# Conv, attention and a routed expert layer on one core: twelve row buffers, roots amid the scatters, the end in eight chunks, and an fp32 product a step that nothing reads

## What is computed

```python
t = t + _L1_attn_ref(_ln_t(t), ...)          # per image: softmax(q k^T / 8) v
t = t + _L1_ffn_ref(_ln_t(t), ...)

def _L1_ffn_ref(x, gate_w, gate_b, w1, w2, w3):
    probs = softmax(x @ gate_w + gate_b)     # 16 experts
    top_probs, top_idx = top_k(probs, 2)
    top_probs = top_probs / sum(top_probs)
    hidden = silu(x @ w1[e]) * (x @ w2[e])   # 64 -> 128, per expert e
    return sum over the two e: top_prob * (hidden @ w3[e])
```

## Time and profile before

| | |
|---|---|
| Median of 3 runs | 452.91 us (451.58 to 456.62) |
| The profiled execution | 452.74 us, span 450.9 |
| PE busy | 359.0 us (80% of the span) |
| DVE busy | 272.1 us (60%) |
| ACT busy | 183.2 us (41%) |
| POOL busy | 162.1 us (36%) |
| Granted PE clock, mean over the span | 0.813 |

### The profile page before, as it was taken

How to read it: one execution, slowest core, us unless ns; L and a number is a source line. 1 busy time by engine, 2 the same in 40 slices (tenths; PEclk the granted TensorE clock), 3 DMA queues, 4 the chain that set the end, 5 groups by cost and what they waited for, 6 DMA issues and landing times. The chain is left out here.

```text
span 450.9 us, 8512 instructions
## 1 busy us (share of the span) xinstructions
PE 359.0 (80%) x2739; PEld 193.0 (43%) x2739; DVE 272.1 (60%) x559; ACT 183.2 (41%) x409; POOL 162.1 (36%) x171
## 2 busy tenths in 40 slices
PE   1689999999999999999998478935507788788760
PEld 0543353433534435344341257735504455465540
DVE  3478977689777798787789656835402232233212
ACT  2683655646556565465630045430012233233220
POOL 2264223234222442224300120457652445445450
PEclk9978999999999999999999979965555555555555
DMA  8769998988978588395880000000023433343315
GB/s 257 312 145 214 287 223 260 302 218 204 221 176 216 128 191 218 76 223 129 195 228 0 1 0 2 9 19 25 24 66 74 94 87 94 91 98 82 94 33 140
DMA packets 55091, 61.50 MB, mean 136 GB/s; under 512 B 22900, under 2 KB 35244, under 8 KB 54928
## 3 DMA queue, kind: packets, MB, share of 16 engines
q1 hardware_dynamic: 45760, 54.30, 47.8%
q10 hardware_dynamic: 6768, 4.62, 3.9%
q0 software_dynamic: 2528, 2.14, 1.6%
HBM read 11.95 MB, written 11.83 MB: 53 GB/s over the span
## 5 line engine op out<-in xcount | busy, mean ns | idle before, releaser
L684 DVE TENSOR_TENSOR prod<-ps_t,a_rep 128x1024 f32<-128x1024 f32 x128 | 152.1, 1219 | 35.4 <-PE ps_t L384 29.3
L791 POOL TENSOR_TENSOR a<-a,mask 128x512 f32<-128x512 f32 (+1 forms) x40 | 46.8, 1171 | 84.3 <-ACT a L544 82.1
L384 PE MATMUL ps_t<-b,vt 32*128 32x512 f32 x512 | 74.7, 650 | 2.0 <-DVE prod L684 1.9
L404 PE MATMUL ps_d<-prod,keep 128*32 128x512 f32 x512 | 69.1, 611 | 1.2 <-DVE prod L684 0.9
L1254 POOL DMA_INDIRECT parts<-y_sb,x_in x47 | 46.0, 978 | 59.0 <-ACT y_sb L1353 42.9
L325 PEld LDWEIGHTS ps_m<-om_r,sel 128*128 128x128 f32 x193 | 29.0, 188 | 75.3 <-ACT mask L522 28.2
L325 PE MATMUL ps_m<-om_r,sel 128*128 128x256 f32 x193 | 49.3, 334 | 0.0
L1500 PE MATMUL ps_xv<-attention_pack,x_in 128*128 128x128 f32 x47 | 21.0, 446 | 31.5 <-DMA x_in<-rows 31.5
L1140 DVE COPY xs<-ps_xv 128x128 f32<-128x128 f32 x47 | 13.7, 291 | 45.7 <-PE ps_xv L1500 45.7
L768 POOL TENSOR_TENSOR om_r<-om_f,om_r 56x512 fp32r<-56x512 f32 x16 | 20.3, 1272 | 56.7 <-ACT om_r L511 56.6
L1345 ACT ACTIVATE gated<-ps_s 128x128 f32<-128x128 f32 x47 | 13.0, 278 | 62.2 <-PE ps_p L1509 62.2
(11 more groups left out here) (151 smaller groups left out, 494.3 us busy)
## 6 DMA issues: line engine op xcount, KB each, us to landing
a_rep<-a SPq DMA_DIRECT2D x128, 256.0 KB, 4.8
rows<-blank SPq DMA_DIRECT2D x8, 1056.0 KB, 7.4
w_in<-in_experts ACTq DMA_DIRECT2D x47, 96.0 KB, 2.0
a_rep<-a SPq DMA_DIRECT2D x32, 128.0 KB, 3.6
x_in<-rows SPq DMA_DIRECT2D x47, 33.0 KB, 1.9
x_in<-rows SPq DMA_DIRECT2D x47, 32.0 KB, 1.8
start<-in_start SPq DMA_DIRECT2D x1, 1344.0 KB, 7.8
both<-parts SPq DMA_DIRECT2D x4, 256.0 KB, 4.0
```

What stands on the lines that cost most here:

```text
L384: mm = pe.matmul(out, vt[par][r, v % 2, :, :, :].rearrange("p j y c -> p (j y c)"), b[par][r, pair_taps(v // 2), :].rearrange("p t x -> p ...
L404: mm = pe.matmul(ps_d[r, :], fold[:, v % 2, :], p, start=v == 0, stop=False, skip_group_check=True)
L684: dve.tensor_tensor(p[:, :, :], t[:, :, :], a_rep[par][:, ms, pair_taps(v // 2), :].rearrange("p m t x -> p m (t x)"), ALU.mult).then_inc( ...
L791: pool.tensor_tensor(v, v, mask[(PAIRS * par + k) % 2][:, 0:wide, :], ALU.mult).then_inc(a_done, 1)
```

## The change

1. `RING`, the number of buffers for rows (`x_in`) and results (`y_sb`) and of the semaphores `x_here` and `sent`, goes from 6 to 12. The weight buffers keep 6 under a name of their own, `WRING`.
2. POOL's `place(q)` becomes `place(q, half)` with four scatters in each half. `power(1, 2)` now stands between the halves of `place(0)`, `power(1, 3)` between those of `place(1)`.
3. The end goes by 8 chunks (`CHUNKS`) of two tiles (`HALF`) instead of 4 of four. SP loads and stores the even chunks, ACT the odd ones, which for that waits for all `sent` itself.
4. In `output(s)`, the wait for `y_done` comes first, then a new fp32 product of two constant tiles, `ident` and `ones` (128x128 each), into a part of PSUM that nothing reads (`ps_go_spare`), and only then the wait for `hidden_done` and the output's product.

```diff
-    RING = 6
+    RING, WRING = 12, 6
     LOADS = 4
+    CHUNKS = 2 * COUPLES
+    HALF = K // 2
...
+        ps_go_spare = [bank_go[:, b, 2 * P:3 * P] for b in two]
...
-            for q in range(COUPLES):
-                sp.dma_start(both[q][:, :, :, :], parts_view[:, K * q:K * (q + 1), :, :]).then_inc(both_in[q], 16)
-            for q in range(COUPLES):
-                sp.wait_ge(finished, q + 1)
-                sp.dma_start(out_view[:, K * q:K * (q + 1), :], t_tok[:, K * q:K * (q + 1), :]).then_inc(stored, 16)
-            sp.wait_ge(stored, 16 * COUPLES)
+            for c in range(0, CHUNKS, 2):
+                sp.dma_start(both[c][:, :, :, :], parts_view[:, HALF * c:HALF * (c + 1), :, :]).then_inc(both_in[c], 16)
+            for c in range(0, CHUNKS, 2):
+                sp.wait_ge(finished, c + 1)
+                sp.dma_start(out_view[:, HALF * c:HALF * (c + 1), :], t_tok[:, HALF * c:HALF * (c + 1), :])\
+                  .then_inc(stored, 16)
+            sp.wait_ge(stored, 16 * CHUNKS)
...
-                for k in range(K * q, K * (q + 1)):
+                for k in range(K * q + HALF * half, K * q + HALF * (half + 1)):
...
-            place(0)
+            place(0, 0)
             power(1, 2)
-            place(1)
+            place(0, 1)
+            place(1, 0)
             power(1, 3)
-            place(2)
-            place(3)
+            place(1, 1)
+            for q in (2, 3):
+                for half in two:
+                    place(q, half)
...
+            for b in range(RING):
+                act.wait_ge(sent[b], 16 * ((STEPS - 1 - b) // RING + 1))
+            for c in range(1, CHUNKS, 2):
+                act.dma_start(both[c][:, :, :, :], parts_view[:, HALF * c:HALF * (c + 1), :, :]).then_inc(both_in[c], 16)
+            for c in range(1, CHUNKS, 2):
+                act.wait_ge(finished, c + 1)
+                act.dma_start(out_view[:, HALF * c:HALF * (c + 1), :], t_tok[:, HALF * c:HALF * (c + 1), :])\
+                   .then_inc(stored, 16)
...
             def output(s):
-                b = s % RING
-                pe.wait_ge(hidden_done, s + 1)
+                b = s % WRING
                 if positive(s - 1):
                     pe.wait_ge(y_done, s - 1)
+                pe.matmul(ps_go_spare[s % 2], ident, ones, start=True, stop=True)
+                pe.wait_ge(hidden_done, s + 1)
                 pe.matmul(ps_y[s % 2], hidden[s % 2][:, :], w_in[b][:, HIDDEN:HIDDEN + C], start=True, stop=True)\
                   .then_inc(y_ps, 1)
```

More of the change, by code:

```diff
@@ L886, in token_stage @@
         x_in = [sb(f"x_in{b}", [P, C + ROW]) for b in range(RING)]
-        w_in = [sb(f"w_in{b}", [P, HIDDEN + C]) for b in range(RING)]
+        w_in = [sb(f"w_in{b}", [P, HIDDEN + C]) for b in range(WRING)]
         xs = [sb(f"xs{b}", [P, P]) for b in two]
@@ L891, in token_stage @@
         y_sb = [sb(f"y_sb{b}", [P, C]) for b in range(RING)]
-        both = [sb(f"both{b}", [P, K, 2, C]) for b in range(COUPLES)]
-        added = [sb(f"added{b}", [P, K, C]) for b in range(COUPLES)]
+        both = [sb(f"both{b}", [P, HALF, 2, C]) for b in range(CHUNKS)]
+        added = [sb(f"added{b}", [P, HALF, C]) for b in range(CHUNKS)]
         bank_xv, bank_s, bank_p, bank_go = ps("ps_xv"), ps("ps_s"), ps("ps_p"), ps("ps_go")
@@ L949, in token_stage @@
         x_here = [sem(f"x_here{b}") for b in range(RING)]
-        w_here = [sem(f"w_here{b}") for b in range(RING)]
+        w_here = [sem(f"w_here{b}") for b in range(WRING)]
         sent = [sem(f"sent{b}") for b in range(RING)]
@@ L958, in token_stage @@
         y_done = sem("y_done")
-        both_in = [sem(f"both_in{b}") for b in range(COUPLES)]
+        both_in = [sem(f"both_in{b}") for b in range(CHUNKS)]
         sum_done = sem("sum_done")
@@ L1151, in finish @@
                 dve.wait_ge(sum_done, q + 1)
-                tokens = t_tok[:, K * q:K * (q + 1), :]
+                tokens = t_tok[:, HALF * q:HALF * (q + 1), :]
                 dve.tensor_tensor(tokens, added[q][:, :, :], tokens, ALU.add).then_inc(finished, 1)
@@ L1219, in _ @@
                     hide(s + 1)
-            for q in range(COUPLES):
-                finish(q)
+            for c in range(CHUNKS):
+                finish(c)
         @block.gpsimd
@@ L1235, in power, with place @@
                     .then_inc(ln_pow[s], 1)
-            def place(q):
+            def place(q, half):
                 pool.wait_ge(staged, 2 * (q + 1))
@@ L1336, in weights_in @@
                     expert_rows.extend(table_values(act, 1, s, (EXPERTS - 1) * P))
-                if positive(s - RING + 1):
-                    act.wait_ge(y_ps, s - RING + 1)
+                if positive(s - WRING + 1):
+                    act.wait_ge(y_ps, s - WRING + 1)
                 act.dma_start(w_in[b][:, :], w_rows[bass.ds(expert_rows[s], P), :]).then_inc(w_here[b], 16)
@@ L1395, in _ @@
             gap_exps(3)
-            for s in range(RING - 1):
+            for s in range(WRING - 1):
                 weights_in(s)
@@ L1402, in _ @@
                 shared(s)
-                if s + RING - 1 < STEPS:
-                    weights_in(s + RING - 1)
+                if s + WRING - 1 < STEPS:
+                    weights_in(s + WRING - 1)
+            for b in range(RING):
[6 more added lines that the diff above has]
+                   .then_inc(stored, 16)
         @block.tensor
@@ L1502, in products @@
             def products(s):
-                b = s % RING
+                b = s % WRING
                 pe.wait_ge(xs_done, s + 1)
-                pe.wait_ge(w_here[b], 16 * uses(s))
+                pe.wait_ge(w_here[b], 16 * (s // WRING + 1))
                 if positive(s - 1):
```

## The result

| | before | after |
|---|---|---|
| Median | 453.97 us of 20 runs (450.62 to 457.30) | 446.46 us of 20 runs (445.18 to 451.97) |
| The profiled execution | 452.74 us, span 450.9 | 446.41 us, span 444.6 |
| Granted PE clock, mean over the span | 0.813 | 0.815 |

After stands to before as 0.984, 95% interval 0.982 to 0.987. The changed kernel is faster by 1.6%, where 8% had been forecast. The whole difference of 6.3 us between the two profiled executions can be laid out from rows.

What follows compares the result with a forecast made beforehand. The prediction took the six-buffer ring and PE at 1.2 GHz to bound the expert steps, with POOL next. Its sum was 452.74 - 33.1 (steps) - 3.5 (roots) - 1.0 (end) = 415.1 us, range 411 to 448.

Steps and rivals of the forecast that it cites:

- What bounds the kernel: Expert steps: six-buffer ring and PE's own work make 2.05 us a step; POOL is next at 1.28.
- Twelve row buffers: Expert steps: way round the ring falls to about 0.7 us a step, so row loads leave the path.
- The extra product's price: Each expert step on PE: 0.43 us at 1.2 GHz, 0.22 us at 2.4 GHz.
- Which level: Expert steps: the added product lifts PE's clock to 2.4 GHz, chance 0.52; steps stage -33.1 us.
- once up stays up: Expert steps: a risen PE clock holds, because the steps contain no long PE standstill.
- The pace once up: Expert steps at 2.4 GHz: POOL binds at 1.28 us a step, 58.9 us for 46 intervals.
- the forecast's 2.5 us for the rise: First 3.5 expert steps: still slow until the clock rises, 0.71 us each over POOL's pace.
- The forecast's sign of PE waiting for DVE ahead of L1533: Expert steps: PE waiting for DVE there would show the high-clock case right; no size given.
- Roots: POOL's scatters: roots placed between them remove its pauses; last scatter starts 3.5 us earlier.
- The end: After the last send: eight chunks on two queues save 1.0 us, bounds 0 and -2.
- The clock stays at 1.2 GHz: Rival for the expert steps: clock never rises, steps 1.99 us, 445.2 us in all; chance 0.30.
- Slower: Rival for the expert steps: clock stays low, product costs up to 0.87 us, 465 us; chance 0.06.

Runs made afterwards that it cites:

- the bridged kernel: Changed kernel plus 60 unread products on PE before the first step, three and two more behind the first two transposes: 414.53 us, 0.914 of before.
- the run with two and then one: Changed kernel with two unread products in each of the first ten steps, one in every later step: 421.10 us, 0.929 of before.
- the run with the burst and no product in the steps: Changed kernel with 52 unread products on PE ahead of the first step and none in the steps: 425.31 us, 0.941 of before.

## Why the prediction was right or wrong

- **What bounds the kernel: right.** Ring and PE shared the 2.05 us a step. With the ring taken away PE's own 1.55 us remains (the runs without the product and with the ring alone), as the earlier trace rows had it. One reading in it was off: the chain of the earlier trace rows comes round every four steps, not six, by the order told at the run with the product alone. 8.05 / 4 is 2.01 us a step, which explains the 2.05; 8.05 / 6 would be 1.34 and bind nothing. With twelve buffers it carries ten steps, 0.8 us each and not 0.7, still under 1.28.
- **Twelve row buffers: right where it counts.** At 1.2 GHz no transpose waits for rows after the first steps. At 2.4 GHz, where the same was forecast, the bridged kernel has two such waits left, 0.8 us in all; they cost nothing, as POOL still sends every 1.28 us.
- **The extra product's price: right.** 0.43 us forecast at 1.2 GHz, 19.7 us over 46 steps measured; the step is 1.985 us, forecast 1.99. At 2.4 GHz steps with none, one and two products go at PE's pace of 0.90, 1.13 and 1.35 us (starts in the timelines of the three kernels), so 0.22 us apiece as forecast; "about 1.0" for a step with one was 0.13 short, but below POOL's 1.28, so it moves nothing.
- **Which level: wrong, and this is the step that failed.** I wrote: "I think it goes up, as a little better than even." It stayed at 0.50 through all 90 us. The only rise I had seen came after nothing but dense products; I carried that over to a step which has 0.43 us of them in 1.99. The rows of before already had two full stretches at 0.50, and I read the new product as enough to change their mix. The waits for rows that broke the stretches did go, as forecast, and that didn't raise it either. In the runs it took two a step (0.86 us in 2.41), or a burst. The other half of the step, "once up stays up", was right, as the run with two and then one shows; but its rows (268 to 270 us with PE 1.45 of 2.00 busy) are rows of holding and say nothing of a kernel that first has to rise. In the sum, the term was -33.1 us and became -4.0.
- **The pace once up: right.** With the clock raised by a burst, the sends take 59.1 us, against 46 x 1.28 = 58.9 forecast, POOL binds, and the time is 414.5 us, against 415.1. That the totals agree so well is in part luck: the forecast's 2.5 us for the rise, which the bridged kernel has under its burst, and its 1.0 off the end, which isn't there, offset each other in part. The forecast's sign of PE waiting for DVE ahead of L1533 isn't there either: PE runs ahead of POOL (steps 1.13 us apart, sends 1.28), and from 345 to 400 us it waits 0.8 us for rows and not for DVE. The mechanism was right; the change as made doesn't set it off.
- **Roots: right.** 3.8 us less between first and last scatter, forecast 3.5; undone in the bridged kernel, 3.6.
- **The end: mis-sized.** -1.0 forecast, 0 measured. DVE's wait for the fifth chunk ends 5.43 us after the first load's issue, and that for the third couple had ended 5.63 us after it; DVE then needs 2.19 us for eight small operations where four large ones took 1.67, and the smaller store gives 0.3 back. The 0.3 us for a small operation was right (0.29, against 0.42 for 128x256), but the forecast counted only the last chunk's two, and eight stand behind DVE's last wait. It also took off half of the 2.04 us of issue; but each of the two queues still has four loads to issue. The Trainium skill (Trainium Kernel Development and Optimization, Key Constraints) says that a second issuing engine saves only issue time; the trace agrees as far as it goes: the landing stays, and two queues took 1.93 and 2.00 us for four loads each, as long as SP alone for four of twice the size (2.04), so what the second queue saved went into the doubled number of loads.
- **The rivals.** "The clock stays at 1.2 GHz" was given 445.2 us and a chance of 0.30; 446.46 was measured. Its own terms: steps -3.0 forecast, -4.0 measured (of which 0.7 because the last two sends are 1.28 us apart and not 1.99); roots -3.5, -3.8; end -1.0, 0.0; the other 1.5 us lie ahead of the first scatter and of the first send. "Slower" fell: switching between 64 and 128 rows costs nothing beyond the 0.43. In the chance of "faster", 0.52 + 0.12 + 0.20 is 0.84 already, so 0.83 with an edge on top doesn't add up; nothing hangs on it.
- **The two rules on TensorE's clock.** The Trainium skill (TensorE: Matmul & The Clock Gate, Part 1) says that activity of PE releases the clock. Read as busy time, the trace disagrees again, now over 90 us: PE busy 10.00 of 10.00, clock 0.50. Part 4 says that transposes don't count as PE being busy in the same way; with a transpose in every step here the clock rises under two products and is held by one, so a transpose a step doesn't keep it down by itself. Whether one product would raise it without the transpose is open, since no run took the transpose out.

## What to carry to other kernels

A stretch in which PE is shown busy all the time is no sign that its clock will rise: look at what was streamed ahead of an earlier rise, and ask separately what raises it and what only holds it. Work that nobody reads, put there to hold a clock, costs its whole duration if the clock isn't up and the engine is the bound, so the raising belongs ahead of the stage, bridged over every pause up to its first real product. Even then look at every execution: three of 21 came out long here. Two edits at the same bound don't add: here a wait was cover for the added product, and the same change took that wait away.

## What the runs showed of the hardware

- Raising and holding differ: one 128x128 fp32 product in a step of 1.985 us did not raise the clock in 47 steps, but held it over more than thirty steps of 1.28 us once two a step, or a burst, had raised it. Without any, the steps of the traced execution held it for some 14 us and then lost it for good.
- A pause ahead of the steps can cost the whole stage: in the run with the burst and no product in the steps, with PE idle for 1.92 us behind the burst and then waiting again, the clock fell as the first step began, and the 47 steps that followed stayed at 0.50. With the product in the steps and 0.52 us idle there, the one traced execution kept it.
- Halving loads and spreading them over two queues left their landing where it was (5.43 against 5.63 us after the first issue), and put half a microsecond more of DVE work behind its last wait (2.19 against 1.67 us).
